# The row scaling of both normalisations, by VectorE or by ScalarE

## What is computed

```python
def _layernorm(x, axis=-1, eps=1e-05):
    m = jnp.mean(x, axis=axis, keepdims=True)
    v = jnp.var(x, axis=axis, keepdims=True)
    return (x - m) / jnp.sqrt(v + eps)

h = tok(x) @ W.T + b                     # frames t, t+3, t+6, 768 -> 256
h = h + attn(_layernorm(h))              # 16 heads, causal, softmax
h = h + ffn(_layernorm(h))               # 4 experts, top 2, gelu, 256 -> 1024 -> 256
```

## Time and profile before

| | |
|---|---|
| median of 3 runs | 1739.21 us (1738.99 to 1742.22) |
| the profiled execution: its time | 1728.33 us |
| its span in the trace | 1726.6 us |
| mean granted TensorE clock | 0.937 of full speed |
| TensorE busy | 1523.0 us |
| VectorE busy | 1101.6 us |
| ScalarE busy | 707.3 us |
| GpSimd busy | 836.9 us |

### The profile page before, as it was taken

The page is one execution under the profiler, slowest core; times in us unless marked ns, Lnnn a source line. Parts: engine busy times, 40 slices in busy tenths (PEclk is TensorE's granted clock), DMA queues, the critical chain, the costliest instruction groups (busy, mean ns, idle before and its releaser), DMA issues.

```text
span 1726.6 us, 33232 instructions
## 1 busy us (share of the span) xinstructions
PE 1523.0 (88%) x10648; PEld 1185.3 (69%) x10648; DVE 1101.6 (64%) x3477; ACT 707.3 (41%) x1464; POOL 836.9 (48%) x912
## 2 busy tenths in 40 slices
PE   6598898997988988988978777899999999999997
PEld 5364474564564654744745434889999999999997
DVE  3367777677687787687776650755555555555554
ACT  1135644634545545445445443233333333333332
POOL 5315435635536546447356342165564544444445
PEclk9689998999999998999999877999999999999998
DMA  3623635635536536436436764265645546455451
GB/s 109 149 55 98 153 101 146 150 94 164 143 90 181 129 104 174 122 111 179 116 110 167 216 217 146 76 201 183 210 166 185 197 154 208 170 171 189 165 200 38
DMA packets 166972, 256.24 MB, mean 148 GB/s; under 512 B 30484, under 2 KB 97998, under 8 KB 166800
## 3 DMA queue, kind: packets, MB, share of 16 engines
q1 hardware_dynamic: 108816, 166.66, 33.0%
q10 hardware_dynamic: 34368, 50.33, 9.1%
q0 software_dynamic: 23616, 37.12, 7.6%
HBM read 173.92 MB, written 75.29 MB: 144 GB/s over the span
## 4 chain that ended last, share of the span: by engine, by line
PE 51%; DVE 13%; issue 12%; DMA 10%; SPq 5%; POOL 4%; ACT 3%; ACTq 0%; DVEq 0%; POOLq 0%
PE yb L1521 14%; PE l1b L1505 13%; PE pab L1341 8%; PE pvb L1453 5%; PE mxb L1409 4%; PE stb L1428 4%; DVE unused L1040 4%; DMA qk_s<-parts 3%; DMA qst<-negp 3%; SPq L593 2%; POOL xs L698 2%; DVE mxp L1043 2%; SPq L561 1%; PE rb L1470 1%; ACT hf L943 1%
## 5 line engine op out<-in xcount | busy, mean ns | idle before, releaser
L857 ACT ACTIVATE prob<-stb 124x496 f32<-124x496 f32 (+2 forms) x832 | 398.0, 505 | 407.8 <-PE stb L1428 378.4
L1040 DVE CUSTOM_DVE_ANT_0 unused<-mxb,mask_row 124x372 bf16<-124x372 f32 (+4 forms) x768 | 352.2, 484 | 72.7 <-PE mxb L1409 68.9
L1409 PE MATMUL mxb<-kst,qst 96*124 96x372 bf16 (+4 forms) x1024 | 315.9, 341 | 84.4 <-DVE mxp L1040 52.9
L1428 PE MATMUL stb<-qst,kst 99*124 99x372 bf16 (+4 forms) x1024 | 310.1, 336 | 40.9 <-ACT prob L857 19.1
L1521 PE MATMUL yb<-w2p,hp 128*128 x2448 | 335.3, 282 | 12.1 <-DVE yo L1296 11.7
L1505 PE MATMUL l1b<-x2T,w1s 128*128 128x384 f32 x1632 | 339.9, 344 | 1.2 <-DVE x2T L1250 1.2
L1521 PEld LDWEIGHTS yb<-w2p,hp 128*128 128x128 f32 x2448 | 320.8, 189 | 22.6 <-issue 22.6
L943 ACT ACTIVATE hf<-l1b,b1c 128x384 f32<-128x384 f32 x272 | 158.3, 582 | 350.2 <-PE l1b L1505 307.2
L1505 PEld LDWEIGHTS l1b<-x2T,w1s 128*128 128x128 f32 x1632 | 277.9, 190 | 1.5 <-DVE x2T L1250 1.4
L1409 PEld LDWEIGHTS mxb<-kst,qst 96*124 96x124 bf16 x1024 | 138.7, 144 | 175.0 <-DVE mxp L1040 94.7
L1282 DVE CAST hp<-hf 128x384 fp32r<-128x384 f32 x272 | 105.3, 387 | 236.4 <-ACT hf L943 189.5
(11 more groups left out here) (178 smaller groups left out, 1492.9 us busy)
## 6 DMA issues: line engine op xcount, KB each, us to landing
w1s<-ws SPq DMA_DIRECT2D x34, 2048.0 KB
qk_s<-parts SPq DMA_DIRECT2D x64, 279.0 KB
xg<-xs SPq DMA_DIRECT2D x34, 396.0 KB
kst<-qk_s SPq DMA_DIRECT2D x32, 279.0 KB, 3.7
qst<-qk_s SPq DMA_DIRECT2D x32, 279.0 KB, 5.2
wraw<-in_w_all ACTq DMA_DIRECT2D x32, 256.0 KB
ws<-whi ACTq DMA_DIRECT2D x32, 256.0 KB
ws<-wlo ACTq DMA_DIRECT2D x32, 256.0 KB
```

Of the source, the lines that this page charges most:

```text
L857: act.activation(dst, src, ACT.Exp, scale=DH ** -0.5).then_inc(exp_done, 1)
L1040: done = dve.tensor_tensor_reduce(out=unused[:, n % 2, e * w:(e + 1) * w], in0=src, in1=mask_row[:, T - w:T], scale=1.0, scalar=-3.0e38, o ...
L1409: done = nc.tensor.matmul(out, qst[g % NG][0:ROWS, h + e, TT * i:TT * i + TT], kst[g % NG][0:ROWS, h + e, k0:k0 + w], start=True, stop=True)
L1428: done = nc.tensor.matmul(out, kst[g][:, h, TT * j:TT * j + TT], qst[g][:, h, q0:q0 + w], start=True, stop=True)
```

## The change

VectorE no longer scales the rows. It writes the negated mean, `shift` = -mean, beside `veps` (one more instruction on 124x6 for each norm). GpSimd, after the power, multiplies `shift` by `rstd` (one more instruction). ScalarE then computes `rstd` x h1 + `shift` for each tile, with scale and bias taken per row, in the place of the list at which VectorE stood. That is done for `xn` and for `xrow`, 48 instructions each over the program. The first one of each six has the waits that VectorE had, now on ScalarE's queue. The gate's first VectorE instruction gets a wait for GpSimd's two steps. The order of the loads at the front is the same in both kernels. The diff, cut where it repeats for the second norm:

```diff
@@ GpSimd @@
-                        pool.wait_ge(veps_ready, a + 1)
+                        pool.wait_ge(veps_ready, 2 * (a + 1))
                         pool.tensor_tensor(rstd[:, :], veps[:, :], power[:, :], ALU.pow).then_inc(rstd_ready, 1)
+                        pool.wait_ge(rstd_ready, 2 * (a + 1) - 1)
+                        pool.tensor_tensor(shift[:, :], shift[:, :], rstd[:, :], ALU.mult).then_inc(rstd_ready, 1)
...
@@ ScalarE @@
+                    if kind == "xn":
+                        if n == 0:
+                            act.wait_ge(rstd_ready, 2 * (a + 1))
+                            if later(a):
+                                act.wait_ge(turn_full, a * 4)
+                        act.activation(xn[:, n, :], h1[:, n, 0:D], ACT.Identity, scale=rstd[:, n:n + 1],
+                                       bias=shift[:, n:n + 1]).then_inc(xn_ready, 1)
+                    if kind == "scale2":
+                        if n == 0:
+                            act.wait_ge(rstd2_ready, 2 * b)
+                            if later(b - 1):
+
+                                act.wait_ge(scattered, (b - 1) * TOP * NT * 16)
+                        act.activation(xrow[:, n, 0:D], res[:, n, 0:D], ACT.Identity, scale=rstd2[:, n:n + 1],
+                                       bias=shift2[:, n:n + 1]).then_inc(xrow_ready, 1)
...
@@ VectorE @@
+                            dve.tensor_scalar(shift[:, :], mv[:, :, 0], -1.0, None, ALU.mult).then_inc(veps_ready, 1)
                             dve.tensor_scalar(veps[:, :], mv[:, :, 1], EPS, None, ALU.add).then_inc(veps_ready, 1)
-                    if kind == "xn":
-                        if n == 0:
-                            dve.wait_ge(rstd_ready, a + 1)
-                            if later(a):
-                                dve.wait_ge(turn_full, a * 4)
-                        dve.tensor_scalar(xn[:, n, :], h1[:, n, 0:D], mv[:, n, 0:1], rstd[:, n:n + 1],
-                                          ALU.subtract, ALU.mult).then_inc(xn_ready, 1)
...
-                        dve.tensor_scalar(xrow[:, n, 0:D], res[:, n, 0:D], mv2[:, n, 0:1], rstd2[:, n:n + 1],
-                                          ALU.subtract, ALU.mult).then_inc(xrow_ready, 1)
...
                         if n == 0:
+                            dve.wait_ge(rstd2_ready, 2 * b)
```

More of the change, by code:

```diff
@@ L370, in layer @@
         rstd = sb("rstd", [TT, NT])
+        shift = sb("shift", [TT, NT])
         vaug = sb("vaug", [TT, NT, NH, DH + 1])
@@ L403, in layer @@
         rstd2 = sb("rstd2", [TT, NT])
+        shift2 = sb("shift2", [TT, NT])
         logit = sb("logit", [TT, NT, NE])
@@ L690, in emit @@
                     if kind == "norm2":
-                        pool.wait_ge(veps2_ready, b)
+                        pool.wait_ge(veps2_ready, 2 * (b))
                         pool.tensor_tensor(rstd2[:, :], veps2[:, :], power[:, :], ALU.pow).then_inc(rstd2_ready, 1)
+                        pool.wait_ge(rstd2_ready, 2 * (b) - 1)
+                        pool.tensor_tensor(shift2[:, :], shift2[:, :], rstd2[:, :], ALU.mult).then_inc(rstd2_ready, 1)
                     if kind == "scatter":
@@ L1081, in emit @@
                         dve.wait_ge(aggr2_done, b * NT)
+                        dve.tensor_scalar(shift2[:, :], mv2[:, :, 0], -1.0, None, ALU.mult).then_inc(veps2_ready, 1)
                         dve.tensor_scalar(veps2[:, :], mv2[:, :, 1], EPS, None, ALU.add).then_inc(veps2_ready, 1)
[L1083 to L1088, removed]
-                        dve.tensor_scalar(xrow[:, n, 0:D], res[:, n, 0:D], mv2[:, n, 0:1], rstd2[:, n:n + 1],
-                                          ALU.subtract, ALU.mult).then_inc(xrow_ready, 1)
                     if kind == "gate":
```

## The result

The changed kernel takes 1712.65 us (median of four runs, 1712.2 to 1718.38) against 1739.1 us before (four runs, 1738.36 to 1742.22): a ratio of 0.987, 95% interval 0.984 to 0.990. Run again beside other experiments, the same kernel gave 0.989 (0.982 to 0.996). The forecast was 1716 us in a range of 1702 to 1737 us. The profiled execution went from a span of 1726.6 to 1710.3 us, 16.3 us less, where the sum had said 23.3. The medians are 26.5 us apart, as the profiled execution of the kernel before (1728.33 us) was a fast one of its kind; the two traces locate 16.3 us and not the rest. All ratios leave out executions over 1.5% slower than the fastest of the same kernel; there is one, of 1737.4 us, of the kernel with doubled rows.

A forecast was written before the change was run, and what follows sets the result against it. VectorE was taken to bound the row-scaling stretches (16.88 of 17.80 us busy). 6 x (1.9 + 0.8 + 0.6) = 19.8, plus 1.5, 0, 0 and 2.0, made 23.3 us: 1705.0, scaled to 1715.8 us; range 1702 to 1737.

The forecast's parts named there:

- xn: First norm's rows leave VectorE in bodies 2 to 7: 1.9 us won for each body (ends 1.0 and 2.6).
- The clock: With less TensorE idling before it, the `pvb` product may run at 2.4 GHz: 0.6 us a body (0 to 1.2).
- xrow: Second norm's rows leave VectorE in bodies 2 to 7, ScalarE handing half back: 0.8 us each (-0.5 to 1.6).
- The new wait: ScalarE's first `xn` waits for GpSimd's `rstd` and `shift`, the product taking 0.25 us; costs nothing where it stands.
- The first body: Without `proj` and `xrow`, VectorE waiting for TensorE now and then: 1.5 us won (ends 0.5 and 3).
- The front: Six `xn` rows at the start: 0 won, TensorE's second pair of transposes within 0.3 us of 43.18 us.
- The last body: Its `xrow` stretch ends at a chain of transfers, `wraw` taking 9.36 us before `wsplit`: 0 won.
- After it: Behind the last body, two groups of three `xrow` on the chain move to ScalarE: 2.0 us won (1 to 3).
- ScalarE the bound: Rival: rows in bodies 2 to 7 delay exps TensorE waits for; 16 us slower, 1755 us, chance 0.11.
- Nothing moves: Rival: VectorE is relieved but transfers or TensorE end last anyway; 1739 us, within 2, chance 0.14.
- Full relief: Rival: ScalarE hides its rows wholly and the clock comes back; 35 us won, 1704 us, chance 0.17.
- Two signs of being wrong: TensorE's score waits for `prob` rising by over 10 us; the `xrow` stretch staying at 10.8 us or growing.

The follow-up runs named there:

- doubled rows: Changed kernel with ScalarE making five of the six rows of each norm twice in the bodies; ratio 0.987 to the kernel before.
- `xn` alone: Kernel before with only the first norm's rows moved to ScalarE, the second norm's staying on VectorE; ratio 0.991.
- the padded kernel: Changed kernel with one more unused VectorE instruction at each of the six xn places of bodies 1 to 7; ratio 0.9975 to the kernel before.
- `xrow` alone: Kernel before with only the second norm's rows moved to ScalarE, the first norm's staying on VectorE; ratio 1.001.

## Why the prediction was right, by its steps

**xn, right: 1.9 forecast, 1.68 measured.** The stretch went from 17.86 to 16.18 us, VectorE has 14.4 us in it (13.9 forecast), the wait before the third transposes is gone, the 16 `pvb` matmuls take under 2 us. ScalarE's instruction takes 0.60 us beside others, 595 ns (`xn`) and 598 ns (`xrow`) on average, where 589 had been worked out from two rows. The Trainium skill (ScalarE: Activation LUTs, What ACT_TABLE_LOAD costs) gave an estimate of 585 ns; the measurements are 10 and 13 ns above it. The agreement within 4 ns that I had noted is that of the worked-out 589 ns; the two rows of 128x384 by themselves lie 14 and 17 ns below the Trainium skill's figures for them. My reading of the chain had two slips that change nothing: it holds all six `xn`, one with 0.10 us, and 2.6 us between VectorE's pieces are "issue". The added VectorE work shows that the cause was the one named.

**The clock, right in kind and sized too low: 0.6 forecast.** I took half of a possible 1.2 us. The product alone gives 0.92 us in each body on average (2.37 to 1.45), and between the second `veps` and the output's store 1.47 us went, of which 1.42 us went with `xn` alone too. So the term was 0.9 to 1.4 us, about twice what I took. That it does not go with VectorE's load, the padded kernel showed.

**xrow, the term that failed in part: 0.8 forecast.** From the output's store to the weight load 0.73 us went, but 0.30 us of it went with `xn` alone too. Over this stretch and the one before it, `xrow` adds 0.49 us a body to what `xn` alone gives. Then 2.3 us came back at once with the blocked issue, which no step had. `xrow` alone gives no time that can be told from none. The step that failed is the one that let ScalarE hand half of VectorE's gain back and saw nothing else late next: the sum counted the work of the engines, and not that ScalarE's DMA issues stand in the same row. The distance of 6.0 us from the store to the load stood in the trace of before; a faster stretch could only shorten it.

**The new wait, right.** GpSimd's product takes 0.20 us (0.25 forecast). ScalarE waits 1.07 us for it, and its next exp starts at the same distance from `veps` as before: 603.71 - 601.46 = 2.25 us, against 610.49 - 608.24 = 2.25 us.

**The first body, wrong: 1.5 forecast, nothing.** The same two score products of TensorE, at 118.09 and 159.63 us before and at 118.78 and 160.42 us after, are 41.54 and 41.64 us apart. A stretch of 43 us of it, from the same event on in both traces, first before and then after:

```profile
117.00:160.00 43.00, 37.59 (x277) 25.26 (x275) 31.06 (x108) 20.16 (x43) 15.74 (x21) 0.96 0.17 58
```

```profile
117.70:160.70 43.00, 38.56 (x277) 26.25 (x275) 28.20 (x103) 22.66 (x49) 15.74 (x22) 0.92 0.17 58
```

VectorE is busy 2.9 us less. TensorE's idle time did fall, from 5.4 to 4.4 us, but its clock was 0.92 in place of 0.96, and its work took 1.0 us longer. Its third transposes, first before and then after:

```profile
141.91 0.54 PE L1363 MATMUL pab<-ident,xn 124*128 124x124 f32 x3 [0.78 <-DVE xn L1013]
```

```profile
142.43 0.83 PE L1372 MATMUL pab<-ident,xn 124*128 124x124 f32 x3
```

Two stretches of 5 us around them, again before and after:

```profile
138.00:143.00 5.00, 3.14 (x17) 1.86 (x16) 4.32 (x15) 2.98 (x7) 3.18 (x4) 1.00 0.01 2
143.00:148.00 5.00, 4.45 (x26) 1.72 (x25) 2.68 (x10) 1.47 (x4) 1.23 (x1) 0.66 0.47 157
```

```profile
138.70:143.70 5.00, 3.59 (x14) 2.14 (x13) 3.79 (x12) 4.05 (x10) 2.40 (x3) 0.75 0.00 0
143.70:148.70 5.00, 5.00 (x28) 2.38 (x27) 2.68 (x10) 1.58 (x5) 1.96 (x2) 0.57 0.45 159
```

The wait for `xn` is gone here too, but the clock fell ahead of the transposes and stayed down longer. So the step that failed was to take TensorE's wait as won: the clock took it back. Why it fell in this body and not in the six later ones is not shown.

**The front, near:** 0 forecast, +0.7 measured up to the first score product (98.51 us before, 99.20 after); TensorE's second transposes came at 43.42 us (43.18 before), within the 0.3 us forecast. **The last body:** 0 forecast, -0.5. **After it, low:** 2.0 forecast, 3.3 measured. The wait of the earlier trace rows fell from 3.17 to 2.20 us:

```profile
1091.21 0.22 PE L1406 MATMUL pab<-rowsum,earlier 124*124 124x4 bf16 x1 [2.20 <-DVE rowsum L1140]
```

**The sum** was 7.0 us too large against the profiled execution: 6.2 of it in the six bodies (19.8 forecast, 13.6 measured), 2.6 in the front and the first body, less 1.8 behind it. And the median still came within 3.4 us of 1716. Some of that is luck: single executions spread by more than the miss, and two misses, the clock and the blocked issue, had opposite signs. *ScalarE the bound* is refuted by the doubled rows. *Nothing moves* is what the median says of `xrow` alone, though its stretch did get shorter. *Full relief* fell at the same place as `xrow`.

**Two signs of being wrong showed all the same.** TensorE's scores were not to wait over 10 us more for `prob`; by the pages they waited 34.4 us in place of 19.1. And the `xrow` stretch was not to stay as long or grow: from the exp behind the first copy of `parts` to the one behind the fourth it is 12.37 us (620.41 to 632.78), where it was 10.71 (630.45 to 641.16). The blocked issue stands in both. So the total came out right although the half with `xrow` did not go as forecast.

## What to carry to other kernels

Moving work off an engine paid here where that engine was busy nearly all of a stretch (16.9 of 17.9 us) and paid nothing in the first body, where it was idle 12 of 43 us and a lower clock took back what little TensorE's waits gave. Its share of the whole says neither. When a stretch gets shorter, list every transfer that its engines issue and the distance of each from the large transfer ahead of it on the same queue: that distance shrinks with the stretch. And to take a stall away is not to gain it: ask first what it holds back, as here, by all the traces suggest, it kept one large store behind another queue's smaller and urgent one.

## What the runs showed of the hardware

- An issue on ScalarE's queue can block ScalarE itself. Behind a store of 755 KB by 1.1 us it took 5.4 to 10.7 us, behind one of 744 KB by 5.3 us 1.0 to 4.5 us, by 5.7 us 0.8 to 1.2 us, by 5.8 us (doubled rows) 2.4 to 3.6 us, by 6.0 us 0.34 us, and 0.33 us at 5.3 us when only half of the store was ahead. So it goes with what the queue still has to move, and not with the time alone.
- A store on ScalarE's queue can delay one on SyncE's. SyncE's last store of `parts` was ready for its load after 2.5 to 4.8 us, and after 6.3 to 9.7 us where ScalarE's issue of the store of `h1` began over 0.3 us before the end of SyncE's.
- TensorE's clock can fall in one body and not in the next on the same instructions: with a wait of 1.21 us ahead of them the 16 `pvb` matmuls took 1.54 to 2.68 us in 23 of 24 bodies, without it 1.44 or 1.45 us in 59 of 60; in the first body of the changed kernel they took 2.59 us without a wait for `xn`.
- A VectorE row scaling beside a GpSimd instruction took 0.94 us, and ScalarE's took 0.59 or 0.60 us each in the same stretch of the changed kernel.
